# A four-stage fp32 image kernel on one core: the first stage's preparation moved off GpSimd, its depthwise convolutions summed in PSUM, its quotients with an operand in PSUM

## What is computed

```
g  = relu(bn(dwconv(h, wg)));  g1 = relu(bn(dwconv(h, wg1)))      # two depthwise 3x3
gy, gx = sobel(h)
Dx = 1/(gy*gy/4 + 1);  Dy = 1/(gx*gx/4 + 1)
ux = 0.5*(roll(g,1,W) - roll(g,-1,W));  vy = 0.5*(roll(g1,1,C) - roll(g1,-1,C))
Ax, Ay = g*DT, g1*DT;  Bx, By = Dx*DT, Dy*DT;  E = (ux+vy)*DT
D = 1/(1 + 2*Bx + 2*By)
cm_x, cp_x = -Ax+2*Bx, Ax+2*Bx;  cm_y, cp_y = -Ay+2*By, Ay+2*By;  c0 = 1 - 2*Bx - 2*By
for _ in range(5):
    h_new = D*(c0*h_prev - 2*E*h + cm_x*roll(h,1,W) + cp_x*roll(h,-1,W)
               + cm_y*roll(h,1,C) + cp_y*roll(h,-1,C)) + D*2*DT*f
```

## Time and profile before

| | before |
|---|---|
| time, median of 3 runs | 1036.42 us (1035.8 to 1038.41) |
| the profiled execution's own time | 1035.26 us |
| its span in the trace | 1033.2 us |
| VectorE busy | 848.9 us (82%) |
| TensorE busy, matmuls | 843.9 us (82%) |
| GpSimd busy | 590.7 us (57%) |
| ScalarE busy | 569.7 us (55%) |
| TensorE clock granted, mean | 0.926 |

### The profile page before, as it was taken

How to read it: one execution, slowest core, us unless ns; L and a number is a source line. 1 busy time by engine, 2 the same in 40 slices (tenths; PEclk the granted TensorE clock), 3 DMA queues, 4 the chain that set the end, 5 groups by cost and what they waited for, 6 DMA issues and landing times.

```text
span 1033.2 us, 8216 instructions
## 1 busy us (share of the span) xinstructions
PE 843.9 (82%) x2690; PEld 421.4 (41%) x2690; DVE 848.9 (82%) x657; ACT 569.7 (55%) x953; POOL 590.7 (57%) x262
## 2 busy tenths in 40 slices
PE   3986998977288898899889599897738889889955
PEld 2432443433144445446445244343314334545633
DVE  5999887268999898998997978636899999899841
ACT  3733332146748886688575332303684878668802
POOL 2444996020668686877354789501065979677730
PEclk8996999989689999999999899998967999999977
DMA  3000000002344454445100100000113545444411
GB/s 100 1 0 0 0 0 1 0 0 56 79 129 163 139 186 144 144 161 143 44 0 1 20 0 0 0 1 0 56 46 102 176 151 183 143 143 162 146 39 20
DMA packets 33206, 74.35 MB, mean 72 GB/s; under 512 B 15753, under 2 KB 15889, under 8 KB 33169
## 3 DMA queue, kind: packets, MB, share of 16 engines
q1 hardware_dynamic: 31760, 72.58, 21.7%
q0 software_dynamic: 320, 1.05, 0.4%
q10 hardware_dynamic: 1088, 0.26, 0.1%
HBM read 70.73 MB, written 3.15 MB: 72 GB/s over the span
## 4 chain that ended last, share of the span: by engine, by line
PE 42%; DVE 38%; ACT 7%; issue 6%; POOL 6%; DMA 0%; DVEq 0%; SPq 0%; POOLq 0%; ACTq 0%
DVE arena L1498 11%; PE ps L672 9%; PE ps L444 9%; PE ps L564 8%; ACT arena L789 5%; DVE ps L1493 4%; PE ps L433 3%; PE ps L666 3%; POOL arena L332 3%; DVE arena L1457 3%; PE ps L450 2%; DVE arena L1355 2%; POOL dr L315 1%; PE ps L534 1%; DVE arena L1487 1%
## 5 line engine op out<-in xcount | busy, mean ns | idle before, releaser
L332 POOL TENSOR_TENSOR arena<-arena 128x1024 f32<-128x1024 f32 x128 | 304.2, 2383 | 113.9 <-DVE arena L1498 60.7
L1498 DVE TENSOR_TENSOR_SCAN arena<-arena,ps 128x1024 f32<-128x1024 f32 x128 | 289.6, 2281 | 18.0 <-POOL arena L332 8.2
L564 PE MATMUL ps<-arena,mat 128*128 128x512 f32 x512 | 251.7, 616 | 8.8 <-POOL arena L332 7.9
L789 ACT ACTIVATE arena<-arena 128x128 f32<-128x128 f32 (+4 forms) x346 | 146.4, 493 | 106.2 <-DVE arena L1425 75.7
L789 ACT ACTIVATE arena<-arena,Amat 128x1024 f32<-128x1024 f32 x128 | 146.1, 1144 | 88.7 <-DVE arena L1498 85.1
L564 PEld LDWEIGHTS ps<-arena,mat 128*128 128x128 f32 x512 | 95.7, 197 | 90.8 <-issue 68.5
L672 PE MATMUL ps<-arena,mat 128*128 128x512 f32 x240 | 106.3, 592 | 0.0
L1493 DVE TENSOR_TENSOR ps<-arena,ps 128x1024 f32<-128x1024 f32 x72 | 87.2, 1210 | 7.7 <-PE ps L534 5.7
L789 ACT ACTIVATE arena<-ps 128x1024 f32<-128x1024 f32 (+2 forms) x58 | 53.7, 934 | 67.3 <-PE ps L433 22.0
L444 PE MATMUL ps<-arena,diag 128*128 128x512 f32 x192 | 86.6, 609 | 2.1 <-ACT arena L789 2.1
L534 PE MATMUL ps<-arena,sel 96*128 96x512 bf16 x144 | 45.5, 401 | 49.5 <-DVE arena L1498 49.5
(11 more groups left out here) (169 smaller groups left out, 1351.2 us busy)
## 6 DMA issues: line engine op xcount, KB each, us to landing
arena<-bc_rows SPq DMA_DIRECT2D x128, 512.0 KB, 3.8
out<-arena SPq DMA_DIRECT2D x28, 64.0 KB, 2.2
xres<-x POOLq DMA_DIRECT2D x4, 256.0 KB, 5.1
bc_rows<-ROWS SPq DMA_DIRECT2D x8, 128.0 KB, 1.9
xres<-x SPq DMA_DIRECT2D x4, 256.0 KB, 4.3
convw<-conv_w SPq DMA_DIRECT2D x1, 576.0 KB
mat<-mats SPq DMA_DIRECT2D x1, 448.0 KB, 3.5
inw<-in_w SPq DMA_DIRECT2D x1, 256.0 KB
```

What stands on the lines that cost most here:

```text
L332: tt(HC[s % 2], HS[s % 2], CB[s % 4], ALU.mult).then_inc(S("hc"), 1)
L564: last = mm(half(PS[3], n), ident, half(HC[s % 2], n), start=first, stop=True, skip_group_check=True)
L789: return nc.scalar.activation(out_, in_, func, bias=bias, scale=scale, accum_out=accum_out)
L1498: nc.vector.tensor_tensor_scan(HS[q], DA[q], PS[q][:, :], 0.0, ALU.mult, ALU.add).then_inc(S("scan"), 1)
```

## The change

The preparation's products leave GpSimd: the Sobel sums of pair 1, the product of the squares, both products with D, and the source of pair 1 become VectorE's (nine operations in each half). GpSimd keeps three: the source of pair 0 and the previous field of both pairs. The convolutions are summed in one PSUM tensor each: ScalarE writes tap 0 there, VectorE adds taps 1 and 2 there, TensorE then accumulates taps 3 to 8 onto it, and `relu` reads it; the four `merge` operations of each half go. Before ScalarE writes, TensorE once writes each of the banks (`write_all`, two bf16 matmuls). The denominator, its reciprocal and the fractions pass through the PSUM tensor of the first convolution (`den_ps`), so that each operation from the second on has at most one tensor operand in SBUF. The order on VectorE, ScalarE and TensorE is written anew. The core of the diff:

```diff
         def conv_ps(h, k, w):
-            return PS[1] if h > 0 and k == 1 and w == 1 else PS[2 * k + 1 - w]
+            if h > 0:
+                return [[PS[0], PS[1]], [PS[3], PS[1]]][k][w]
+            return PS[2 * k + 1 - w]
...
+        def den_ps(h, k):
+            return PS[0] if h > 0 and k == 0 else PS[2 * k + 1]
...
-            def source_and_previous(h, k):
-                a = A[k]
-                f_in = frm(a["fz"])[:, 1:33, 1:33]
                 pool.wait_ge(S("a_P0"), 2 * h + k + 1)
-                tt(img(a["Sc"]), img(a["Sc"]), f_in, ALU.mult).then_inc(S("a_Sc"), 1)
-                pool.wait_ge(S(f"a{k}_G"), 2 * h + 2)
+                pool.wait_ge(S("a_Pm"), 2 * h + k + 1)
                 pool.wait_ge(S("a_div"), 2 * h + k + 1)
-                tt(img(a["g"]), img(a["P0"]), f_in, ALU.mult).then_inc(S(f"a{k}_g"), 1)
+                tt(img(a["g"]), img(a["P0"]), frm(a["fz"])[:, 1:33, 1:33], ALU.mult).then_inc(S(f"a{k}_g"), 1)
...
+                source(h, 0)
+                previous_product(h, 0)
+                previous_product(h, 1)
...
             def depthwise(h, k, w, n):
-                pe.wait_ge(S("a_fz"), 2 * h + k + 1)
-                pe.wait_ge(S(f"group{k}"), g_var(h, 0))
-                if h > 0:
-                    pe.wait_ge(S("scan"), SCANS * h)
-                    pe.wait_ge(S("y_read"), ONE + 4 * h)
-                    if k == 1 and w == 1:
-                        pe.wait_ge(S("a_merge"), 4 * h + 1)
-                last = conv_taps(conv_ps(h, k, w), lambda tap: blk(diag, 9 * (1 - w) + tap), frm(A[k]["fz"]),
-                                 n, range(OFF_PE, 9), OFF_PE)
+                pe.wait_ge(S("a_tap"), (OFF_PE - 1) * (4 * h + 2 * k + w + 1))
+                for tap in range(OFF_PE, 9):
+                    dy, dx = tap // 3, tap % 3
+                    last = mm(half(conv_ps(h, k, w), n), blk(diag, 9 * (1 - w) + tap), frm(A[k]["fz"])[:, dy + HB * n:dy + HB * n + HB, dx:dx + W],
+                              start=False, stop=(tap == 8), skip_group_check=True)
                 if n == 1:
                     last.then_inc(S(f"a_conv{w}"), 1)
+
+            def write_all(ps):
+                for n in range(2):
+                    last = mm(half(ps, n), sel[:, 0:P], sel[:, 0:BANK], start=True, stop=True, skip_group_check=True)
+                last.then_inc(S("a_open"), 1)
...
+                if h + 1 < HALVES:
+                    pe.wait_ge(S("scan"), SCANS * (h + 1))
+                    write_all(PS[1])
                 sum_of(h, SCANS - 1)
+                if h + 1 < HALVES:
+                    depthwise(h + 1, 0, 0, 0)
                 out_proj(h, 3)
...
-            def first_taps(h, k):
+            def first_tap(h, k, w):
                 act.wait_ge(S("a_fz"), 2 * h + k + 1)
-                for name, w in [("g1", 0), ("g", 1)]:
-                    col = V_WG + 9 * (1 - w)
-                    av(img(A[k][name]), frm(A[k]["fz"])[:, 0:H, 0:W], ACT.Identity, vecs[:, col:col + 1]).then_inc(S("a_tap0"), 1)
+                if h > 0:
+                    if k == 0:
+                        act.wait_ge(S("scan"), SCANS * h - 1 + w)
+                        if w == 1:
+                            act.wait_ge(S("a_open"), 5)
+                    elif w == 0:
+                        act.wait_ge(S("y_read"), ONE + 4 * h)
+                    else:
+                        act.wait_ge(S("a0_gg1"), 2 * h + 2)
+                else:
+                    act.wait_ge(S("a_open"), 2 * k + 1 + w)
+                col = V_WG + 9 * (1 - w)
+                av(img(conv_ps(h, k, w)), frm(A[k]["fz"])[:, 0:H, 0:W], ACT.Identity, vecs[:, col:col + 1]).then_inc(S("a_tap0"), 1)
...
             def relu(h, k, w):
                 t = A[k]["g1" if w == 0 else "g"]
                 c = 2 - 2 * w
-                act.wait_ge(S("a_merge"), 4 * h + 2 * k + w + 1)
-                av(t, t, ACT.Relu, par[:, c:c + 1], par[:, c + 1:c + 2]).then_inc(S(f"a{k}_gg1"), 1)
+                act.wait_ge(S(f"a_conv{w}"), 2 * h + k + 1)
+                av(t, conv_ps(h, k, w)[:, :], ACT.Relu, par[:, c:c + 1], par[:, c + 1:c + 2]).then_inc(S(f"a{k}_gg1"), 1)
...
             def fractions(h, k):
-                a, newton = A[k], S("a_newton")
+                a, newton, den = A[k], S("a_newton"), den_ps(h, k)[:, :]
 
                 dve.wait_ge(S("a_rec"), 4 * h + 2 * k + 2)
-                tt(a["sden"], a["sden"], a["R"], ALU.mult).then_inc(newton, 1)
+                tt(den, den, a["R"], ALU.mult).then_inc(newton, 1)
                 dve.wait_ge(newton, 4 * h + 2 * k + 1)
-                stt(a["R"], a["sden"], -2.0, a["R"], ALU.add, ALU.mult).then_inc(newton, 1)
+                stt(den, den, -2.0, a["R"], ALU.add, ALU.mult).then_inc(newton, 1)
                 dve.wait_ge(newton, 4 * h + 2 * k + 2)
-                stt(a["Dc"], a["XY"], -1.0, a["R"], ALU.mult, ALU.mult).then_inc(S("a_D"), 1)
-                stt(a["Kx"], a["Y"][:, 0:L], -2 * DT, a["R"], ALU.mult, ALU.mult)
-                stt(a["Ky"], a["X"][:, 0:L], -2 * DT, a["R"], ALU.mult, ALU.mult).then_inc(S("a_K"), 1)
+                stt(a["Dc"], den, -1.0, a["XY"], ALU.mult, ALU.mult).then_inc(S("a_D"), 1)
+                stt(a["Kx"], den, -2 * DT, a["Y"][:, 0:L], ALU.mult, ALU.mult)
+                stt(a["Ky"], den, -2 * DT, a["X"][:, 0:L], ALU.mult, ALU.mult).then_inc(S("a_K"), 1)
```

196 lines of the change are left out of this document (96 added, 100 removed).

## The result

| | before | after |
|---|---|---|
| time, median | 1036.11 us (1035.52 to 1038.41, 4 runs) | 1018.59 us (1018.47 to 1021.03, 4 runs) |
| ratio, 95% interval | | 0.9824 [0.9808, 0.9839] |
| span of the profiled execution | 1033.2 us | 1016.6 us |

The forecast was 1018.0 us, a ratio of 0.982. The page of the changed kernel, busy time by engine and the chain by engine, answers to the earlier trace rows: VectorE has ten instructions more and is busy for 30 us less.

A forecast was written before the change was run, and what follows sets the result against it. VectorE was taken to bound the preparation, waiting for GpSimd instructions where both inputs lie in SBUF. First half 13.7 plus second half 4.7 make 18.4 us less, so 1018.0 us from the median; range 1010 to 1027.

The forecast's parts named there:

- without a break: First half before the change: VectorE is continuously the engine the iterations wait for; they begin at 101.57 us.
- The walk: First half, step by step through ScalarE, VectorE and TensorE: the iterations begin at 87.9 us instead of 101.57.
- First half, 13.7 less: First preparation: iterations begin at 87.9 us instead of 101.57, so 13.7 us less.
- TensorE stays ahead: First half: relu 76.3, rolls to 78.8, second divergence done at 84.6 us, where VectorE needs it at 86.7.
- Second half, 4.7 less: Second preparation: 12.5 us less in the last stretch plus 0.9 for the clock, minus 8.7 of lateness: 4.7 us less.
- 8.7 us of lateness: Second half: the last convolution's first part starts at 563.1 us instead of 554.45, 8.7 late.
- Its own sign: Prediction wrong if convolutions run longer at the low clock, or the second half's convolutions end over 9 us late.
- Second half gives nothing: Rival: the second half's relay of waits gives no gain or takes some; 1022.7 us, up to 1027; chance 0.22.
- More: Rival: full clock at the first convolution (2.9 us) and half the second half's lateness gone; 1010.7 us; chance 0.15.
- Slower: Rival: convolutions wait for their taps and TensorE runs at the low clock; up to 1059 us; chance 0.05.
- PSUM operands held: Rival: VectorE operations with one PSUM operand are still held by GpSimd's remaining three; 13.2 us more, 1031; chance 0.05.
- 2.6 us more for reading PSUM: Skill's rule of extra fixed cycles for a PSUM source, 40 VectorE operations: 1020.6 us; the prediction did not adopt it.

The follow-up runs named there:

- e7: Changed kernel with denominators and quotients kept in SBUF and the products with D back on GpSimd: 1027.31 us, ratio 0.9902.
- e1: Changed kernel with the products with D moved from VectorE back to GpSimd: 1016.97 us, ratio 0.9812.
- e4: Changed kernel with ScalarE's four squares of field 0 ahead of the first convolution's relu in the first half: 1018.06 us, ratio 0.9811.
- e6: Changed kernel with all eight moved products of each half back on GpSimd, PSUM convolutions and quotients kept: 1017.15 us, ratio 0.9806.
- first profile: Profiled execution of the changed kernel as first measured, with no further edit: span 1016.6 us, median 1018.59 us.
- second profile: Profiled execution of the changed kernel timed a second time, with no further edit: median 1018.50 us, ratio 0.9832.
- e5: Changed kernel, second half: TensorE does the second part of pair 0's convolution g ahead of the layer norm's transposes: 1013.35 us, ratio 0.9766.
- e3: Kernel before the change, with only the same eight products of each half moved to VectorE: 1028.83 us, ratio 0.9915.
- e8: Changed kernel with squares ahead of relu and second-half work reordered on TensorE, VectorE and ScalarE to remove TensorE's pauses: 1007.84 us, ratio 0.9717.
- e2: Changed kernel with denominators, logarithm input and fractions in SBUF instead of PSUM: 1024.58 us, ratio 0.9876.

## Why the prediction was right, point by point

- **What bounds the kernel.** Right, and shown: VectorE lost time where both its inputs lay in SBUF and GpSimd was at work (e7 against e1, same line, 3.38 against 1.21 us). One reading was off: VectorE is not "without a break" what the iterations wait for. Before, it stood still for 1.96 us just ahead of them (`100.43 1.22 DVE L1404 TENSOR_TENSOR arena<-arena,ps 128x1024 f32<-128x1024 f32 x1 [1.96 <-PE ps L483]`), for a divergence behind rolls at the low clock, so not all of the 20 us of holding was on the path. The walk does not use it.
- **First half, 13.7 less.** Measured: `products` 13.3 us earlier, at 88.25, though the half began 0.57 later. The steps stand: taps done 25.1 (measured 26), first wait of VectorE 3.9 (3.67), convolutions' end 75.0 (75.8), second divergence 84.6 (85.0), `last_source` not held (L1397 1.22 us; GpSimd's product beside it took 3.07 instead).
- **A step that was wrong without cost:** "TensorE stays ahead." From 59.6 on VectorE depends on the third convolution's relu; e4 shows that VectorE can't be earlier there. That VectorE's own work ends at the same moment is luck; it is why the sum came out.
- **Where the gain is from.** The prediction took the moved products and the PSUM operands as one remedy and did not split them. The runs do in part: the moved products alone 8 to 9 us, the PSUM convolutions with the new order alone 8 to 9, PSUM convolutions, PSUM quotients and new order together all of it (e6), the products on top of them nothing that can be told. What the order gives by itself is not shown.
- **Second half, 4.7 less.** Measured 3.4. The mis-sized term is the 8.7 us of lateness of the last convolution's first part: it was 10.1 (550.18 - 482.59 against 554.45 - 496.95). Up to X3's transposes the steps were right in the first profile (7.3 forecast, 6.9 measured). Two things were missing. First, more time at the low clock: the prediction charged it to the layer norm's transposes and the projection alone, but another 1.7 us falls on what follows X3's pause, 6.64 for 5.32 and 1.48 for 1.07. Second, ScalarE's passes behind X3's transposes, its copy and the four squares, stand ahead of the relu that the second denominator waits for. In the second profile the extra low-clock time falls ahead of X3's transposes, which are 8.0 late; the convolution behind them has the full clock, but the relu waits for ScalarE's squares, and the last convolution's first part starts at 550.09 all the same. That the pause of 6.82 causes the extra low-clock time is argued from e5: without that pause both rows are at the full clock, and the lateness is 4.2 (544.99 - 483.34 against the 57.50 of before).
- **Its own sign.** The prediction called itself wrong if the second half's convolutions ended more than 9 us late. They ended 10.2 late (the last part starts at 558.94 and takes 5.31 us; 564.25 - 482.59 against 568.43 - 496.95), and VectorE waited 7.15 us ahead of the second denominator instead of about 5. So for the second half that sign came; it cost 1.3 us, little enough for the sum to stand.
- **Sum.** 18.4 forecast, 16.6 in the span, 17.5 between the medians. That the median is only 0.6 off is in part luck, for the same sum is 1.8 off in the span. Of these 1.8, 1.3 are the term above and 0.2 are in the first half; the rest is a stretch behind the second preparation that is 1.2 longer, less 0.9 between the two. It lasts 435.2 us in the profile of before and 435.6 to 437.8 in the twelve others, e3's among them. No run aimed at it; its cause stays open.
- **The rivals.** "Second half gives nothing" did not come: it gives 3.4 us, and with e8's order 15. "More" did not come either: the first three convolutions took as long as before (33.71 us, 33.93 before), low clock at the start included, and the second half's lateness did not halve. "Slower" neither: beyond the start the low clock cost the convolutions about 1 us (1.3 in the first profile, 0.9 in the second). "PSUM operands held" is out by e1. The 2.6 us more for reading PSUM did not show: quotient operations with a PSUM input have rows of 1.21 to 1.23 us, those between SBUF tensors 1.22, and two taps take 2.6 us whether they add in PSUM or in SBUF.

## What to carry to other kernels

Before moving work off a slower engine, look at what stands beside each of its instructions: here a GpSimd product cost VectorE 0.8 to 2.2 us beside an operation with two SBUF inputs and nothing beside one that reads PSUM, so changing one operand's place can be worth as much as moving the work, and the two are no sum. Where an edit removes an engine's wait and the time stays, look for the same wait further down (3.67 us at 44.30 became 3.51 at 60.75). A new pause of TensorE can be paid twice, as idle time and as slow matmuls behind it (e2: 4.49 us and 1.7). Here ready work in the place of a pause gave 5 us, and the order of TensorE's list, with small moves in VectorE's and ScalarE's, some 11 in all, on top of the 17.5 of the change.

## What the runs showed of the hardware

- An operation with two SBUF inputs is held by a GpSimd product even if its result goes to PSUM (L1383 in e1: 3.37 us).
- Either side may be the one that waits, and both can: beside the held operations of e7 two GpSimd products took 6.56 us, in e1 5.66 and 4.68, and in the changed kernel it was GpSimd's product that waited (3.07 us).
- The length of the last pause alone does not tell TensorE's clock. X3's transposes stand behind pauses of 2.30 us in two profiles of the changed kernel and of 2.43 in e5: they took 1.48, 1.07 and 1.06. The granted clock over 533 to 541 us was 0.79 in the first and 1.00 in the second, and 1.00 over 528 to 536 in e5.
- The start-up costs TensorE a varying amount: the first three convolutions took 32.4 to 33.9 us, start to start, in eleven profiles in which the same 72 rows stand in the same order. The granted clock over 26 to 30 us was 0.69 in the shortest (e6, 7 rows) and 0.50 in the longest (e5, 5 rows). The clock column can miss this: both profiles of the changed kernel read 1.00 there, with 5 and 6 rows.
